# Filler matrix products on TensorE at the stage seams and inside the attention prologues of a two-layer transformer

## The reference, cut to what matters

```
layer 0:  ada = silu(c) @ W_ada + b_ada            # six rows: shift, scale, gate, twice
          h = layernorm(x) * (1 + scale) + shift
          q, k, v = heads(h @ W_qkv + b_qkv)
          x = x + gate * (softmax(q k^T / sqrt(18)) v @ W_proj + b_proj)
          h = layernorm(x) * (1 + scale2) + shift2
          x = x + gate2 * (gelu(h @ W_fc1 + b_fc1) @ W_fc2 + b_fc2)
layer 1:  the same attention half; then
          logits = h @ w_gate;  top 2 of 4 experts, softmax of the two logits
          x = x + gate2 * sum_e cw[e] * (gelu(h @ w1[e] + b1[e]) @ w2[e] + b2[e])
```

## Time and profile before

| | us |
|---|---|
| median of 3 runs | 1550.79 |
| lowest and highest run | 1545.91, 1553.46 |
| profiled execution, its own time | 1542.11 |
| its span from first to last instruction | 1540.4 |
| PE busy | 1392.7 (90%) |
| DVE busy | 1114.8 (72%) |
| ACT busy | 811.8 (53%) |
| POOL busy | 631.9 (41%) |
| mean granted TensorE clock | 0.929 |

### The profile page before, as it was taken

One profiled execution on the slowest core, in us unless ns is written; L12 is line 12 of the kernel. 1 busy time (PEld: TensorE's weight loads), 2 busy tenths in 40 slices (PEclk: granted clock), 3 DMA queues, 4 the chain that ended last, 5 costly groups with the idle time before them and its releaser, 6 DMA issues. The chain is left out here.

```text
span 1540.4 us, 27402 instructions
## 1 busy us (share of the span) xinstructions
PE 1392.7 (90%) x9863; PEld 852.2 (55%) x9863; DVE 1114.8 (72%) x1807; ACT 811.8 (53%) x1533; POOL 631.9 (41%) x870
## 2 busy tenths in 40 slices
PE   5989999999997889989799999999986499999995
PEld 3753333333333678967433333333345499999994
DVE  3557899999991646766589999999839365666653
ACT  3623778877885431245157877877851133333331
POOL 2145433553000435534479877988005212121121
PEclk7975999999998989989679999999998699999998
DMA  7576434544001178427743211330039577676773
GB/s 188 164 188 111 116 85 110 137 108 72 3 3 33 51 229 281 162 57 241 172 60 50 48 32 23 48 49 3 4 131 341 186 231 206 206 233 183 240 197 77
DMA packets 93836, 194.63 MB, mean 126 GB/s; under 512 B 35734, under 2 KB 63448, under 8 KB 90716
## 3 DMA queue, kind: packets, MB, share of 16 engines
q1 hardware_dynamic: 61802, 117.93, 24.2%
q0 software_dynamic: 31600, 73.00, 21.5%
q10 hardware_dynamic: 306, 2.00, 0.6%
HBM read 127.27 MB, written 66.68 MB: 126 GB/s over the span
## 5 line engine op out<-in xcount | busy, mean ns | idle before, releaser
L1099 DVE TENSOR_REDUCE att_neg_max<-att_for_max 128x1 f32<-128x1024 f32 x512 | 617.1, 1222 | 52.6 <-PE att_for_max L1177 47.1
L1084 ACT ACTIVATE att_probs<-att_scores 128x512 f32<-128x512 f32 x1002 | 541.8, 604 | 173.5 <-PE att_scores L1216 166.0
L1228 PE MATMUL att_out<-att_probs,V 128*32 128x256 f32 (+1 forms) x3232 | 310.5, 456 | 2.9 <-ACT att_OZ L1070 1.9
L1177 PE MATMUL att_for_max<-att_KS,att_QS 54*128 54x512 f32 x640 | 243.3, 455 | 6.8 <-DVE att_neg_max L1099 6.8
L1216 PE MATMUL att_scores<-att_QS,att_KS 56*128 56x512 f32 x618 | 225.4, 450 | 0.9 <-DMA att_QS<-att_neg_max_rows 0.9
L2093 ACT ACTIVATE experts_gelu<-experts_proj,experts_b 128x256 f32<-128x256 f32 x171 | 81.1, 474 | 207.9 <-PE experts_proj L2162 186.1
L1177 PE MATMUL att_for_max<-KS,QS 54*128 54x512 f32 x384 | 165.5, 530 | 13.2 <-DVE att_neg_max L1099 10.1
L2162 PE MATMUL experts_proj<-experts_x_parts,w_parts 128*128 128x256 f32 (+1 forms) x1197 | 173.6, 285 | 1.4 <-DVE experts_x_parts L1902 1.4
L2051 POOL DMA_INDIRECT sums_of_experts<-experts_y,experts_rows x38 | 61.2, 1610 | 259.4 <-DVE experts_y L1938 253.6
L1216 PEld LDWEIGHTS att_scores<-att_QS,att_KS 56*128 56x128 f32 x618 | 94.3, 184 | 131.4 <-ACT att_probs L1084 115.2
L2162 PEld LDWEIGHTS experts_proj<-experts_x_parts,w_parts 128*128 128x128 f32 (+1 forms) x1197 | 157.4, 190 | 5.4 <-issue 5.4
(11 more groups left out here) (267 smaller groups left out, 1980.5 us busy)
## 6 DMA issues: line engine op xcount, KB each, us to landing
w_parts<-w_parts SPq DMA_DIRECT2D x19, 2304.0 KB
qk_halves<-qkv_qk_parts SPq DMA_DIRECT2D x40, 288.0 KB
w_parts<-w_parts SPq DMA_DIRECT2D x4, 2592.0 KB, 26.1
slot_rows<-mlp_blank_rows SPq DMA_DIRECT2D x2, 5145.0 KB
att_QS<-qk_halves POOLq DMA_DIRECT2D x120, 72.0 KB, 4.6
att_KS<-qk_halves POOLq DMA_DIRECT2D x60, 144.0 KB, 5.2
w_parts<-w_parts SPq DMA_DIRECT2D x19, 432.0 KB
experts_rows<-slot_rows SPq DMA_DIRECT2D x19, 294.0 KB, 10.3
```

Of the source, the lines that this page charges most:

```text
L1084: nc.scalar.activation(PR[st % 2][:, j, :], score_bank(st, n), ACT.Exp, scale=SCALE).then_inc(exp_done, 1)
L1099: nc.vector.tensor_reduce(negm[half][:, c:c + 1], psM[ring % 2][:].rearrange("p a n -> p (a n)"), AX_X, ALU.max, negate=True).then_inc(rin ...
L1177: last = nc.tensor.matmul(psM[ring % 2][:, keys, :], QS[s][rows, half, p, t * P:(t + 1) * P], KS[s][rows, p, keys * BLK:(keys + 1) * BLK], ...
L1228: last = nc.tensor.matmul(psO[32 * j:32 * j + 32, n0:n1], T.V[:, g, k, 32 * j:32 * j + 32], PR[st % 2][:, j, n0:n1], start=(k == 0 and n0 ...
```

## The change

A helper `keep_busy` issues n products of `sel_parts` by itself, repeated four times to 512 columns, into a PSUM bank that nothing reads before it is overwritten. It is called: in `qkv_stage` 4 times ahead of the first turn and 3 behind it; in the attention prologue 3 behind each unit and 4 more at its end; 12 behind L1289; in `project_stage` 24 ahead of the turn of block 3 and 6 behind it (a PSUM bank of its own is added); 10 at the end of `mlp_stage`; 16 in `experts_stage` ahead of `turn_rows(0)`. There a new semaphore `nearly_out` is raised by POOL when it has issued the rows of the last tile but one, and PE waits for it, and the waits that stood behind `turn_rows(0)` now stand ahead of it. In all 234 products are added. No other engine gets work, but for the one semaphore increment on POOL.

```diff
+def keep_busy(nc, T, bank, n):
+
+    many = T.sel_parts[:].rearrange("p (o n) -> p o n", o=1).broadcast_to([P, 4, P])
+    for _ in range(n):
+        nc.tensor.matmul(bank.rearrange("p (o n) -> p o n", o=4), T.sel_parts[:], many, start=True, stop=True)
...
@@ qkv_stage, tensor
             pe.sem_inc(N.xn_ready, 1)
+            keep_busy(nc, T, psV[0][:], 4)
             norm_transposes(nc, pe, N, T, psT, 0, T.xn0[l])
+            keep_busy(nc, T, psV[0][:], 3)
             pe.wait_ge(w_ready, KC)
@@ attention_stage, tensor
             for q in range(UNITS + AHEAD):
                 unit(q)
+                keep_busy(nc, T, psO[:], 3)
                 if early:
                     ada(q)
                 if q == UNITS + 1:
                     turn(0)
+            keep_busy(nc, T, psO[:], 4)
...
             nc.tensor.matmul(psM[ring % 2][:, 0, :], T.sel[:], OZ[HALVES - 1][:], start=True, stop=True
                              ).then_inc(ring_ready, 1)
+            keep_busy(nc, T, psO[:], 12)
@@ project_stage
+        psF = banks("idle", 1)[0]
...
                 if i + 1 < NBLK:
                     project(i + 1)
+                else:
+                    keep_busy(nc, T, psF[:], 24)
                 norm_transposes(nc, pe, N, T, psT, i)
+            keep_busy(nc, T, psF[:], 6)
@@ mlp_stage, tensor
             for k in range(NBLK * NF - LAG, NBLK * NF):
                 down(k)
+            keep_busy(nc, T, psH[0][:], 10)
@@ experts_stage
+        nearly_out = sem("nearly_out")
...
                             HR[:, j0 + t, :], None).then_inc(row_out, 16)
+                    if j0 + t == TILES - 2:
+                        pool.sem_inc(nearly_out, 1)
...
-            turn_rows(0)
             pe.wait_ge(added, TILES)
             pe.wait_ge(route_steps, seen["counts_read"])
             pe.wait_ge(route_steps, seen["experts"])
+            pe.wait_ge(nearly_out, 1)
+            keep_busy(nc, T, psP[RING][:], 16)
+            turn_rows(0)
             for b in range(EBLOCKS):
```

## The result

The changed kernel is slower: 1597.61 us median against 1550.04, a ratio of 1.0318 with a 95% interval of 1.0270 to 1.0365. I had forecast 1531 us. The profiled execution took 1597.87 us, its span is 1596.2.

The account below looks back on a forecast made before the run. DVE's reductions were taken to bound the attention prologues, half-clock PE the first steps. Gains of 2.3 + 2.3 + 1.5 + 1.9 + 2.0 + 0.8 + 0.8 + 2.2 = 13.8 us gave 1528.3 or 1537.0; forecast 1531, range 1521 to 1546.

Parts of the forecast that it names:

- What bounds the kernel: Half-clock stretches total 194.7 us; DVE's 1.22 us reductions pace the attention prologues, while PE is waited for in first steps.
- Part 1: First steps of both attentions: at full clock reductions go every 1.25 us, gaining 6.3 and 3.8 us.
- Part 2: Attention prologues: fillers cost about 2 us until the clock rises, 1.5 us in layer 1, 4 us in layer 0.
- its three groups: Layer 0's prologue: the condition's products, two warm groups at 0.8 us each and a cold one at 1.6.
- Part 3: Stage seams: fillers keep the clock up across pauses, each counted at about half between nothing and full worth.
- Behind attention, at the turn and at the MLP: Seams from attention to projections, 1.5 us gained, and at the last turn and MLP start, 1.9 us.
- qkv of layer 1: Start of layer 1's qkv stage: fillers hide behind ACT if warm; gain taken as 0.8 us.
- qkv of layer 0: Start of layer 0's qkv stage: starts cold, then mostly warm products; gain 2 us, from -1.5 to 3.1.
- Experts' tiles: Seam from attention to experts: 3.2 us of cold work, worth 1.6; gain taken as 0.8 us.
- Experts' first block: Sixteen cold fillers just fit before the rows come, so turn and first products run warm; gain 2.2 us.
- Rival 4: Prologues: the clock never rises and PE becomes the bound at 2.25 us a unit; 1577 us, chance 5%.
- rival 3: Prologues: the clock swings, half of the 22 units at the cold price; 1550 us, no change, chance 6%.

Follow-up runs that it names:

- paired6: The changed kernel with six products behind every second prologue unit in place of three behind each; ratio 0.9993 to the kernel before.
- long54: seams_only with 46 products on 54 rows in place of 16 on 128 ahead of the experts' first turn; ratio 0.9994 to the kernel before.
- own_rows: The changed kernel with the three products behind every unit on the unit's own weights and 54 rows, not 128; ratio 1.0050 to the kernel before.
- eight: The changed kernel with eight products in place of three behind every prologue unit; ratio 1.0411 to the kernel before.
- seams_only: The changed kernel without the prologues' products, those at the stage seams kept; 1532.3 us beside 1540.1 for the kernel before, ratio 0.9967.
- prologues_only: The changed kernel with the prologues' products alone, the seven other keep_busy calls removed; ratio 1.0420 to the kernel before.
- experts32: seams_only with 32 products in place of 16 ahead of the experts' first turn; ratio 0.9976 to the kernel before.
- after: The profiled execution of the changed kernel with all its fillers, 1597.87 us; median 1597.61 us, ratio 1.0318 to the kernel before.
- burst54: seams_only with the 16 products ahead of the experts' first turn on 54 rows in place of 128; ratio 0.9962 to the kernel before.
- paired8: The changed kernel with eight products behind every second prologue unit in place of three behind each; ratio 1.0022 to the kernel before.
- experts46: seams_only with 46 products in place of 16 ahead of the experts' first turn; ratio 0.9971 to the kernel before.

## Why the prediction was wrong, point by point

**What bounds the kernel: right.** DVE's reductions did set the prologue's pace, and the cold clock there cost next to nothing. The consequence was not drawn: where DVE is the bound, TensorE's clock has nothing to give, and a filler has much to take.

**Part 1, the first steps: 0 of 6.3 + 3.8 us.** The clock did not rise in the prologue, so nothing was gained. The seven reductions of layer 1's first steps take 12.5 us as before (831.03 to 843.53; the earlier trace rows: 12.6). The pace was right: with the clock up, paired6 shows 1.22 us a reduction. That it saves time over the whole attention is not shown: from the first score to its last product paired6 took 355 us in both layers, inside the 348 to 359 of the other traces.

**Part 2, the price of the fillers: this step failed.** The sentence was "So the start costs 2 us, 1 to 3": the clock was to rise within about two units, because six stretches of products had it back after 3.2 to 6.2 us. All six were stretches of full products on 126 or 128 rows, one behind the other. A unit with three fillers is two products on 54 rows, three on 128 and two changes between them, and that did not raise the clock in 68 us. The runs show it from both sides. Products on 54 rows alone never raised it (long54, 20 us; own_rows, 33 us). More fillers behind the same units did (eight), and so did the same fillers with half of the changes and with the units in pairs (paired6). How the rows and the changes weigh against each other in the changed kernel is not settled; no run took away the changes alone.

The price was too low too. A cold unit was forecast at 2.25 us and took 2.73, for the 0.3 us at each change were not in the sum. 22 x (2.73 - 1.27) = 32.1 us is what layer 1 lost, to 0.1 us, and that close by luck: the product leaves out the four fillers ahead of the score (1.7 us), and the first unit, which was warm, took 1.2 us less. In layer 0 it is 37.4: the condition's products came on top, with reductions 4.27 us apart there in place of 2.73. The forecast's 4 us for layer 0 are nearly filled by its three groups (0.8 + 0.8 + 1.6) and the turns, so the 2 us of the start seem to be missing from it. A warm unit was forecast at 1.16 and took 1.52. By that one warm unit, had the clock risen at once, 22 units would still have lost 22 x 0.25 = 5.5 us in each layer, 11 us in all against the 10.1 that part 1 was to bring. This is an estimate; no run held three fillers a unit at full clock.

**Part 3, the seams: right in direction.** Forecast 9.2 us, measured 5 by the ratio of seams_only, whose interval reaches from 0 to 10.
- Behind attention, at the turn and at the MLP (forecast 3.4): the clock held at all three in the changed kernel and in seams_only, and the time up to the MLP fell by 4.8 and 3.6 us. Over the eleven traces that have these fillers it fell by 2.1 to 4.8, with 0.6 in prologues_only, which has none.
- qkv of layer 1 (0.8): the way from the MLP to it fell by 5.8 us, to 125.6. There the MLP's own products were warm from the first, and the pause at the earlier trace rows, behind which the clock fell before, was gone. But the same fillers gave 0.5 us in experts32 (130.9) and 0.8 in eight, and prologues_only has 129.6 with none. So this trace's 5.8 is luck in part.
- qkv of layer 0 (2.0): the clock stayed at 1.00 from the start to 95 us, where it had been at 0.50 for 17 us, and the first unit of attention came at 98.3 us instead of 98.1. Nothing was gained, nor in the ten other traces with these fillers, where it came at 97.1 to 100.7 us. The timeline of ACT near the stage's end shows who was late:

```profile
85.68 0.69 ACT L699 ACTIVATE qkv_qk_parts<-qkv_qk,qkv_b_qk 126x512 fp32r<-126x512 f32 x1 [1.62 <-DMA qk_halves<-qkv_qk_parts]
89.26 0.69 ACT L699 ACTIVATE qkv_qk_parts<-qkv_qk,qkv_b_qk 126x512 fp32r<-126x512 f32 x1 [2.89 <-DMA qk_halves<-qkv_qk_parts]
```

  ACT waits for the stores of the parts, as in the trace of before (4.26 us, up to 89.52), and PE waits for ACT and DVE. This close to the end, the stage goes by its stores.
- Experts' tiles (0.8): 1.6 us here, but the first scatter came 17.5 us behind the first projection in only five of the eleven traces with these fillers and 19.1 to 19.2 behind it in six, as before (19.1).
- Experts' first block (2.2): nothing. The step "raises `nearly_out` near 1204.5", 1.5 us ahead of the last scatter, failed: the products began 4.6 us ahead of it (8.1 in seams_only) and were over 3.56 us before the rows came, and the clock was gone again. In the program the semaphore is raised behind all scatters but the last two, which by POOL's rows would be 2 us ahead of the last; POOL's queue raised it earlier than that, so that it held nothing back, and PE started when DVE let it (below). I had bounded neither that nor what a pause behind the products would do, which part 3 had named as the danger for every other seam.

**The rivals.** Rival 4 is what happened, with a chance of 5%. Its own price (1.0 us a unit) gives 1577; with 1.46 us it would have given 1597. The point made against it, six stretches that rose within 6.2 us, was no evidence about products on 54 rows. The one piece for it, first steps that worked for 12 and 16 us without a rise, was, and I had it in hand. The Trainium skill (TensorE: Matmul & The Clock Gate, part on the clock gate) calls the warm-up a matter of time and not of the number of products; long54 shows that time is not enough either, since a busy PE waited 20 us in vain. The sentence cited for rival 3, on a clock that swings, did not apply in the prologues: there was no swing, only a clock that stayed low.

## What to carry to other kernels

Before filling an engine to raise its clock, ask who waits for it: where another engine is the bound, the most a faster clock gives is the few places where the order turns round, and the filler makes the idle engine the new bound. Take the time that a clock needs to rise from stretches with the same shape of products, rows and changes of tile included, and put filler in long runs rather than between small groups. Filler belongs into pauses that something else bounds, and it has to last up to the end of the pause: one that leaves 2.4 us saved the clock in some executions only. And read what a seam is worth from several traces.

## What the runs showed that I had not expected

**Rows count.** On 54 of 128 rows, TensorE streamed for 20 us, and in own_rows in both halves of the array for 33 us, and stayed at 1.2 GHz.

**The same pause lost the clock or kept it.** All eleven traces with the seam fillers have the pause of 2.43 us ahead of the MLP. The clock held there in four (after, seams_only, burst54, long54). In the seven others it was at 0.50 for 3.4 us around the MLP's start. The first 21 products then took 6.5 to 6.7 us in place of the 5.14 of after, as here in own_rows:

```profile
554.86 6.68 PE L1583 MATMUL mlp_hidden<-hT,w_parts 128*128 128x512 f32 x21 [2.43 <-PEq L119]
```

At the pause of 2.5 us ahead of the projections it fell in four of the eleven, ahead of the turn in none. And behind the burst in the experts it fell 2.0 to 5.1 us after the last product, in the eight traces where it had risen and a pause followed. So part 3's "about half" for such a seam was not far off, and a single trace can't tell what one is worth.

**A change between 54 and 128 rows costs about 0.3 us** cold and 0.2 to 0.3 warm, on top of the products. The Trainium skill (TensorE: Matmul & The Clock Gate, part on row and column tiling) says that a weight load overlaps with products under way only where the rows differ. By that the load at each change would lie bare, and the load there took 0.29 us at half clock. But the sixteen products in the experts, all on the same rows, follow each other in 0.42 us with nothing between. So the trace agrees at the changes alone, and what makes a change differ is not shown.

**POOL's semaphore comes ahead of POOL's rows.** `nearly_out` is raised behind the third-last scatter. In seams_only PE's sixteen products, which wait for it, start at 1185.13 us. A row of DVE and the rows of POOL there:

```profile
1184.71 0.17 DVE L1886 TENSOR_SCALAR experts_expert_of_block<-experts_expert 128x19 int32<-128x19 f32 x1
```

```profile
1184.39 0.96 POOL L2055 DMA_INDIRECT slot_rows<-experts_slot_rows,experts_slots  x1 [0.30 <-issue]
...
1190.72 0.96 POOL L2055 DMA_INDIRECT slot_rows<-experts_slot_rows,experts_slots  x1 [0.30 <-issue]
1191.98 0.96 POOL L2055 DMA_INDIRECT slot_rows<-experts_slot_rows,experts_slots  x1 [0.30 <-issue]
1193.24 0.96 POOL L2055 DMA_INDIRECT slot_rows<-experts_slot_rows,experts_slots  x1 [0.30 <-issue]
```

The scatter behind which it stands in the program starts at 1190.72, 5.6 us later than the products that waited for it; in after it is 2.1 us later (1258.42 against 1256.35). How much earlier still it was raised is not seen, for it was not the last thing that PE waited for. In all eleven traces the products start 0.25 to 0.26 us behind the end of DVE's row above, the experts of the blocks, for which PE waits too. In the trace of before that row ends at 1197.67, 8.4 us ahead of the last scatter. So the start of the burst could have been read from it.

**DVE now and then takes 5.5 us longer for the experts' last routing chain.** In after and in three of the eleven experiments (paired8, burst54, experts46) it took 51.6 to 52.6 us from the first scatter to the last, elsewhere 46.1 to 47.5. The timeline of DVE in after:

```profile
1240.83 0.17 DVE L1804 TENSOR_TENSOR experts_logits<-experts_logits,experts_rstd 128x12 f32<-128x12 f32 x1 [1.23 <-DVE experts_logits L1801]
...
1243.68 0.23 DVE L1817 TENSOR_REDUCE experts_beaten_by<-experts_pairs_upper 128x12 f32<-128x48 f32 x1 [1.14 <-DVE experts_pairs_upper L1814]
...
1245.78 0.17 DVE L1822 TENSOR_TENSOR experts_chosen<-experts_beaten_by,experts_limits 128x12 f32<-128x12 f32 x1 [1.20 <-DVE experts_beaten_by L1820]
```

Each of these follows an operation of its own engine, with 1.1 to 1.2 us between, where the same chain has no such pause in the trace of before. It came with fillers and with 54-row bursts alike, and not in seams_only, so the change isn't shown to cause it. But all four are among the five traces whose first scatter came early, 17.5 us behind the first projection, so a link to that is possible. The cause stays open, and it may be part of why single runs of one kernel lie 15 us apart.
